# A decoder layer and a non-local block: the softmax reciprocals in one DMA, and the order of SyncE's queue

## The reference

```
def attention(q, k, v, mask):                     # 16 heads of 32 columns
    scores = einsum('bhqd,bhkd->bhqk', q, k) / sqrt(32)
    scores = scores * mask - 10000.0 * (1.0 - mask)
    return einsum('bhqk,bhkd->bhqd', softmax(scores), v)

ln  = layernorm(x, ln1_s, ln1_b)
x   = x + merge_heads(attention(split(ln @ w_qkv + b_qkv))) @ w_ao + b_ao
ln  = layernorm(x, ln2_s, ln2_b)
x   = x + merge_heads(attention(ln @ w_q, ctx @ w_kv, cross_mask)) @ w_co + b_co
x   = x + gelu(layernorm(x, ln3_s, ln3_b) @ w1 + b1) @ w2 + b2
# then a non-local block of 1x1 convolutions over x and ctx, with x added at the end
```

## Time and profile before

| what | value |
|---|---|
| median of 3 runs | 2120.47 us (2114.42 to 2125.18) |
| the profiled execution | 2126.38 us, its span 2124.4 us |
| busy PE / PEld / DVE / ACT / POOL | 95% / 75% / 69% / 55% / 26% of the span |
| mean granted TensorE clock | 0.974 |
| busy PE from 1400 us to the end of the span | 717.94 of 724 us |
| DMA packets | 670,396, of which 483,073 under 512 bytes |

### The profile page before, as it was taken

One profiled execution on the slowest core, in us unless ns is written; L12 is line 12 of the kernel. 1 busy time (PEld: TensorE's weight loads), 2 busy tenths in 40 slices (PEclk: granted clock), 3 DMA queues, 4 the chain that ended last, 5 costly groups with the idle time before them and its releaser, 6 DMA issues. The chain is left out here.

```text
span 2124.4 us, 41981 instructions
## 1 busy us (share of the span) xinstructions
PE 2010.5 (95%) x13584; PEld 1589.6 (75%) x13584; DVE 1474.8 (69%) x3874; ACT 1158.1 (55%) x3239; POOL 553.4 (26%) x562
## 2 busy tenths in 40 slices
PE   9998999999998999999999999799999999999998
PEld 8876676766766666767777767577888888888887
DVE  7798888987978877977988988566343544434333
ACT  4387777877867877877877877532111111212111
POOL 1022221221224334233333334134131303213100
PEclk9999999999999999999999999899999999999999
DMA  8445565565466665566566566552212121121201
GB/s 273 152 97 124 131 165 124 118 161 126 117 179 159 174 167 140 154 166 140 154 169 152 146 169 155 134 167 65 65 50 68 49 79 37 67 72 51 62 23 45
DMA packets 670396, 257.42 MB, mean 121 GB/s; under 512 B 483073, under 2 KB 614785, under 8 KB 670209
## 3 DMA queue, kind: packets, MB, share of 16 engines
q1 hardware_dynamic: 670208, 255.12, 46.4%
HBM read 170.56 MB, written 84.41 MB: 120 GB/s over the span
## 5 line engine op out<-in xcount | busy, mean ns | idle before, releaser
L1323 ACT ACTIVATE A_p<-A_p,A_nmax 128x256 f32<-128x256 f32 x1024 | 506.6, 500 | 1.7 <-DVE A_res L1591 1.7
L1615 DVE TENSOR_TENSOR A_p<-A_sc,A_mk 128x1024 f32<-128x1024 f32 x256 | 312.2, 1220 | 156.2 <-DMA exponentials<-A_p 80.6
L1625 DVE CUSTOM_DVE_ANT_0 A_p<-A_p,A_ma 128x256 f32<-128x256 f32 x1024 | 372.9, 418 | 4.7
L836 POOL TENSOR_TENSOR A_ct_l<-A_cx,A_ct_h 128x256 fp32r<-128x256 f32 x128 | 118.7, 927 | 725.7 <-DVE A_nmax L1625 694.6
L1330 ACT ACTIVATE A_pt<-A_tp 128x512 f32<-128x512 f32 x384 | 214.3, 589 | 124.8 <-PE A_tp L1085 124.0
L1085 PEld LDWEIGHTS A_tp<-A_ident,A_p 128*128 128x128 f32 x1536 | 185.7, 148 | 77.2 <-issue 32.3
L1085 PE MATMUL A_tp<-A_ident,A_p 128*128 128x128 f32 x1536 | 231.6, 290 | 1.1 <-DVE A_xt_l L1574 0.7
L1103 PE MATMUL A_banks<-A_pt,A_v 128*32 128x256 f32 x2048 | 151.3, 417 | 78.0 <-DMA A_pt<-exponentials 76.5
L1323 ACT ACTIVATION_READ_ACCUMULATOR A_p<-A_p,A_nmax 128x1 f32 x1024 | 196.9, 192 | 0.0
L1462 ACT ACTIVATE A_mk<-A_tp,A_cols 128x512 f32<-128x512 f32 x62 | 42.7, 689 | 269.0 <-PE A_tp L70 269.0
L1462 ACT ACTIVATE A_ma<-A_tp,A_cols 128x512 f32<-128x512 f32 x62 | 42.8, 690 | 241.4 <-PE A_tp L70 241.4
(11 more groups left out here) (247 smaller groups left out, 5074.2 us busy)
## 6 DMA issues: line engine op xcount, KB each, us to landing
exponentials<-A_p SPq DMA_DIRECT2D x512, 64.0 KB, 2.2
A_pt<-exponentials SPq DMA_DIRECT2D x128, 256.0 KB, 3.8
A_x<-x SPq DMA_DIRECT2D x96, 256.0 KB, 3.8
A_res<-x SPq DMA_DIRECT2D x64, 256.0 KB, 2.9
A_rt<-inverses SPq DMA_DIRECT2D x512, 32.0 KB, 1.9
x<-A_res SPq DMA_DIRECT2D x64, 256.0 KB, 3.4
turned<-A_x SPq DMA_DIRECT2D x240, 64.0 KB, 2.2
inverses<-A_turned_inv SPq DMA_DIRECT2D x512, 1.0 KB
```

Of the source, the lines that this page charges most:

```text
L836: pool.tensor_tensor(ct_l[:, f, part], cx[:, :], f32(ct_h[:, f, part]), ALU.subtract).then_inc(c_lo, 1)
L1323: act.activation(p[:, g % 2, j, t, :], p[:, g % 2, j, t, :], ACT.Exp, scale=-1.0, bias=nmax[:, g % 2, j, t:t + 1], accum_out=rsum[:, g % 2 ...
L1615: dve.tensor_tensor(p[:, g % 2, heads, :, :].rearrange("p j t s -> p j (t s)"), sc[:, heads, :], m, ALU.mult)\
L1625: dve.tensor_tensor_reduce(out=a_, in0=a_, in1=ma[:, b, t, :], scale=-1.0, scalar=BIG, op0=ALU.add, op1=ALU.min, accum_out=nmax[:, g % 2, ...
```

## The change

The reciprocals of a group leave `turned_inv` in one DMA over all 128 partitions, the unused columns included, and the scratch tensor in DRAM grows from 2x8x128 to 2x128x32. For this the sums are kept with the head ahead of the query tile, `rt` is filled in runs of 32 queries, with the two query tiles of a run behind each other, and `scaled` reads it in that order. In SyncE's queue, the writes of row tiles 0 and 1 (`store`) go from slot 5 to slot 6, the block writes of row tile 3 (`store_tile`) come right behind tile 2's in slot 5, and the loads of residual tiles 2 and 3 (`load_res`) go from the middle of slot 6 to its end, behind the writes.

```diff
-        rsum = room.sb("rsum", [P, 2, TPB, HPG])
+        rsum = room.sb("rsum", [P, 2, HPG, TPB])
...
                 wait_apart(sp, inv_t, grp + 1, ld_i, (grp - 1) * HPG * DMA)
-                for n in range(P // 32):
-                    sp.dma_start(inv_dram[g % 2][:, n * 32:(n + 1) * 32], turned_inv[n * 32:n * 32 + TPB * HPG, g % 2, :])\
-                        .then_inc(st_i, DMA)
+                sp.dma_start(inv_dram[g % 2], turned_inv[:, g % 2, :]).then_inc(st_i, DMA)
...
-                wait_apart(sp, st_i, (grp + 1) * (P // 32) * DMA, cx_ok, grp)
+                wait_apart(sp, st_i, (grp + 1) * DMA, cx_ok, grp)
+                blocks = inv_dram[g % 2].rearrange("(n c) s -> n (c s)", c=32).rearrange("(a n) s -> a n s", a=1)
                 for j in range(HPG):
                     rr = slice(j * HD, (j + 1) * HD)
-                    own = inv_dram[g % 2].rearrange("(t j) s -> j t s", j=HPG)[j:j + 1]
-                    sp.dma_start(rt[rr, :].rearrange("p (t s) -> p t s", t=TPB), own.broadcast_to([HD, TPB, P]))\
-                        .then_inc(ld_i, DMA)
+                    own = blocks[:, :, j * TPB * 32:(j + 1) * TPB * 32]
+                    sp.dma_start(rt[rr, :].rearrange("p (n s) -> p n s", n=P // 32),
+                                 own.broadcast_to([HD, P // 32, TPB * 32])).then_inc(ld_i, DMA)
...
                     store_inverses(r, h)
-                    if h == 6 and 0 < k < NU:
-                        for t in range(2):
-                            load_res(k - 1, r - 1, t + 2)
...
-                if by_blocks(k) and h == 4:
-                    store_tile(k, r, 0)
-                    store_tile(k, r, 1)
-                if by_blocks(k) and h == 5:
-                    store_tile(k, r, 2)
...
-                if h == (5 if k < NU else 3) and k:
+                if h == (6 if k < NU else 3) and k:
                     for t in range(2):
                         store(k - 1, r - 1, t)
-                if by_blocks(k) and h == 5:
-                    store_tile(k, r, 3)
+                if by_blocks(k) and h in (4, 5):
+                    store_tile(k, r, 2 * h - 8)
+                    store_tile(k, r, 2 * h - 7)
+                if h == 6 and 0 < k < NU:
+                    for t in range(2):
+                        load_res(k - 1, r - 1, t + 2)
...
-                dve.tensor_tensor(cx[:, :], banks[:, pv[0], 0:S], rt[:, :], ALU.mult).then_inc(cx_ok, 1)
+                in_order = lambda ap: ap.rearrange("p (t n s) -> p t n s", t=TPB, n=P // 32)
+                dve.tensor_tensor(in_order(cx[:, :]), in_order(banks[:, pv[0], 0:S]),
+                                  rt[:, :].rearrange("p (n t s) -> p t n s", t=TPB, n=P // 32), ALU.mult).then_inc(cx_ok, 1)
```

More of the change, by code:

```diff
@@ L1323, in exponential @@
                 act.activation(p[:, g % 2, j, t, :], p[:, g % 2, j, t, :], ACT.Exp, scale=-1.0,
-                               bias=nmax[:, g % 2, j, t:t + 1], accum_out=rsum[:, g % 2, t, j:j + 1]).then_inc(exped, 1)
+                               bias=nmax[:, g % 2, j, t:t + 1], accum_out=rsum[:, g % 2, j, t:t + 1]).then_inc(exped, 1)
             def turned_out(r, h, i):
@@ L1631, in inverses @@
                 dve.wait_ge(exped, (grp + 1) * HPG * TPB)
-                dve.reciprocal(rinv[:, g % 2, 0:TPB * HPG], rsum[:, g % 2, :, :].rearrange("p t j -> p (t j)"))\
+                dve.reciprocal(rinv[:, g % 2, 0:TPB * HPG], rsum[:, g % 2, :, :].rearrange("p j t -> p (j t)"))\
                     .then_inc(inv_ok, 1)
-                wait_apart(dve, inv_ok, grp + 1, st_i, (grp - 1) * (P // 32) * DMA)
+                wait_apart(dve, inv_ok, grp + 1, st_i, (grp - 1) * DMA)
                 dve.transpose(turned_inv[:, g % 2, :], rinv[:, g % 2, :]).then_inc(inv_t, 1)
@@ L1901, in decoder_layer_and_nonlocal @@
     m1t = nc.dram_tensor("m1t", [B, P, S], F32, kind="Internal").ap()
-    inverses = nc.dram_tensor("inverses", [2, TPB * HPG, P], F32, kind="Internal").ap()
+    inverses = nc.dram_tensor("inverses", [2, P, 32], F32, kind="Internal").ap()
     exponentials = nc.dram_tensor("exponentials", [2, MOVED, TPB, S, P], F32, kind="Internal").ap()
```

## The result

| | time, us | ratio to before |
|---|---|---|
| before, 12 runs beside it | 2120.83 (2114.42 to 2132.19) | |
| changed kernel, 12 runs | 2138.03 (2131.18 to 2143.32) | 1.0076, 95% interval 1.0058 to 1.0094 |

The change makes the kernel **0.76% slower**, 17 us. 2100 with 2064 to 2132 was forecast: the direction was wrong and the time lies outside the range. The profiled execution took 2137.21 us, its span 2135.3 us, at a mean granted clock of 0.973 against 0.974.

The account below looks back on a forecast made before the run. PE, 95% busy, was bounded by late A_pt loads in SyncE's queue, 6.85 us a round; 5.5 after: 19 us over 14 rounds, plus 4 elsewhere, less 3 for the clock, gives -20 us: 2100, range 2064 to 2132.

Parts of the forecast that it names:

- slot 6: Slot 6's load of A_pt goes 2.2 us earlier, at 436.2, leaving a stall of 2.3 us of 4.47.
- 0.4 + 0.9: SyncE time freed by the single reciprocal DMA ahead of slot 6's load: 0.4 us in slot 4, 0.9 in slot 5.
- the excess of 2.0 us: Slot 5's two writes took 2.91 us to issue, usually 0.83; the excess was assumed to stay, only 0.9 counted.
- The rival with 2068: Slot 5's long issue disappears too, so slot 6 hardly stalls: 3.4 us a round, about 2068; chance 0.20.
- only these two issues are that long in this slot: Argument for the rival that slot 5's excess goes too: only the two residual writes issue that long there.
- the loads of rt in smaller pieces: Four loads in pieces of 256 bytes instead of 512: at most 0.3 us later landing, on VectorE's scaling; taken as 0.
- The write lands 3.4 us after its issue.: End of slot 6: the first residual load waits for this landing and goes at 445.5, slot 7's A_pt load at 446.5.
- fourth rival: Slower: slot 6's write lands late behind the 512 KB load and PE's clock falls; about 2146, chance 0.22.
- the third term: Clock: a slow stretch in slot 7 mostly runs into the wait; charged 0.2 us a round, 3 us.
- the second term: After slot 7's weighing: 0.6 us of PE idle for the next block, 0.4 us for VectorE's lateness in slots 0 and 1.

Follow-up runs that it names:

- `swap_only`: `one_dma` with the four block writes of row tile 3 ahead of the two residual writes in slot 5, slot 6 as before; 2095.99 us, ratio 0.9883.
- `one_dma`: The kernel before with only the reciprocals changed to one DMA, SyncE's queue in the order of before; 2095.21 us, ratio 0.9883.
- `pair_behind`: The changed kernel with slot 6's 512 KB load moved from ahead of the two writes to between them and the residual loads; 2104.23 us, ratio 0.9924.
- `gap_behind`: `pair_behind` with row tile 0's four block writes right behind slot 4's load of A_pt, in SyncE's idle time; 2081.59 us, ratio 0.9827.
- `write_early`: The changed kernel with slot 6's writes right behind the reciprocals and the residual loads behind the loads of rt; 2109.48 us, ratio 0.9947.
- `tile_in_gap`: `one_dma` with row tile 0's four block writes right behind slot 4's load of A_pt, in SyncE's idle time; 2077.36 us, ratio 0.9801.

## Why the prediction was wrong

**Right: slot 6.** From the end of slot 5 (429.12 after, 428.13 in rows 2) the load of A_pt goes at +7.83 us, forecast +8.07 (436.2), before +10.30. The stall is 2.10 us, forecast 2.3. Over 14 rounds the single DMA alone takes 20.3 us off slot 6 (61.3 to 41.0), 1.45 us a round, forecast 0.4 + 0.9.

**Right: the excess of 2.0 us stays**, on the eight writes L733 (6.12 us, where the same eight take 4.2 in slot 4 of the kernel before). The rival with 2068 is out, by `swap_only` also as an explanation. The prediction's "only these two issues are that long in this slot" holds for round 4 and five others, not for the other eight. The excess is still in slot 5 although three DMAs a slot are gone, and the page has the same 94 transfers and 1.54 MB on the instruction queue as the earlier trace rows. The Trainium skill, "Runtime: NRT & Kernel Launch", section Instruction fetch mechanics, has the crossing of a fetched block mostly hidden; whether this excess is one that isn't hidden, no run here shows.

**Right: the loads of rt in smaller pieces** cost next to nothing. Their median landing is 2.1 us (1.9 in rows 6), inside the 0.3 that was given, and `one_dma` has them and gains 27 us. The 512 bytes of the Trainium skill ("DMA: Bandwidth & Descriptors", section Specifications) decide nothing here: landing rises by 0.2 us where pieces are halved to 256 bytes.

**Wrong, the step that failed: "The write lands 3.4 us after its issue."** It landed 5.3 us after it, and slot 7's load of A_pt went at +20.18 from the end of slot 5, forecast +18.4, so PE weighed at +23.95, forecast +22.3. The 3.4 is a median over 64 writes at different places: those of slot 5 land after 3.1 us in the median, those of slot 7 after 3.9. The trace of before had a place with the neighbours of the new one: in slot 7 the writes stand directly behind two loads of 256 KB. SyncE's timeline in round 5 and the view of the two writes:

```profile
532.60 0.91 SPq L483 DMA_DIRECT2D A_x<-x  x2
533.55 0.91 SPq L501 DMA_DIRECT2D x<-A_res  x2
...
DMA to landing us min/median/max: 5.3/5.4/5.5
```

That is what the two writes of the changed kernel then took. Not every round has it so long: that place has 3.3 to 5.5 us before, and the new one 4.0 to 6.0 with a median of 4.9, and 3.4 is at the low end of the one and below the other. The 4.7 us of the first write in slot 5 of round 4, behind a 512 KB load and four small writes, is of another kind: 2.44 of them are its own long issue (2.91 for the two in the earlier trace rows).

The prediction's fourth rival said it in words ("Writes are the transfers that land latest after a 512 KB load, which stands right in front of them in slot 6") and gave it 0.22, while the forecast's sum used the median. `pair_behind` shows that this term is the loss: with the load gone from in front of the writes, slots 6 and 7 together take 21.75 us a round from the end of slot 5 ((29.5 + 25.8) / 14 + 17.8), forecast 22.3. In the changed kernel they take 23.6. These 1.3 us in 14 rounds are 18 us. That `pair_behind` comes to 2104 us, near the forecast's 2100, is in part luck: its slot 0 costs 20 us more than the forecast has, and slots 6, 7 and 1 to 5 less.

**Wrong, the second term: slot 0, "0.6 us of idle" and 0.4.** It takes 2.15 us a round above the undisturbed slot (30.1 / 14), forecast 1.0: 16 us. Of the 2.15, 0.58 had been there before (8.1 / 14), which the sum didn't look at. The step counted VectorE up to the lower half of the next block and stopped there. Its queue has one more piece that PE waits for, the drain of the second product of slot 7. It stood in the trace of before, right behind the lower half of the earlier trace rows:

```profile
453.67 0.68 DVE L1591 TENSOR_TENSOR A_res<-A_banks,A_res 128x512 f32<-128x512 f32 x1
```

GpSimd's and VectorE's timelines of the changed kernel in round 4:

```profile
450.65 2.49 POOL L790 TENSOR_TENSOR A_res<-A_res,A_o_bias 128x512 f32<-128x512 f32 x2 [11.31 <-DMA A_res<-x]
...
452.01 0.69 DVE L1586 TENSOR_TENSOR A_res<-A_banks,A_res 128x512 f32<-128x512 f32 x1 [4.03 <-POOL A_res L790]
...
454.38 1.22 DVE L1575 TENSOR_TENSOR A_xt_l<-A_e,A_xt_h 128x1024 fp32r<-128x1024 f32 x1
455.52 0.68 DVE L1586 TENSOR_TENSOR A_res<-A_banks,A_res 128x512 f32<-128x512 f32 x1
```

The second drain ends at 456.20 and PE's product begins at 456.25, with the 1.09 us of idle named after it. That is 0.6 us behind the lower half. But over the 14 rounds PE's idle time in slot 0 is only 5.5 us; most of the 30.1 us is time at the lower clock, the third term. `pair_behind` (33.8) and `gap_behind` (29.4) show that slot 0's cost doesn't come from the late write alone: it goes with the loads at the end of slot 6, since the kernels with the loads at the old place have 8.0 to 14.9, and `write_early`, with them in the middle of the slot, 17.1.

**Wrong, the third term: the clock, "0.2 us a round".** The sum took the slow stretch of slot 7 (2.38 us in rows 2) out of the round and charged 0.2 us for a new one. The stretch did not go, it moved. Slots 7 and 0 at the turn from round 3 to 4, before, then in the changed kernel, and there also at the turn from 4 to 5; the third number from the end is the granted clock:

```profile
363.35:374.48 11.13, 11.13 (x77) 8.35 (x77) 6.98 (x24) 6.21 (x17) 2.57 (x2) 0.78 0.71 177
374.48:383.38 8.90, 8.90 (x81) 6.84 (x77) 8.76 (x26) 7.42 (x25) 1.59 (x1) 1.00 0.74 192
```

```profile
359.63:371.77 12.14, 8.97 (x76) 6.92 (x77) 6.17 (x16) 8.22 (x26) 2.45 (x2) 1.00 0.73 188
371.77:384.36 12.59, 12.03 (x77) 9.09 (x77) 10.93 (x35) 6.76 (x19) 2.19 (x3) 0.73 0.60 155
...
453.07:463.32 10.25, 9.16 (x77) 6.92 (x77) 10.12 (x34) 6.14 (x19) 1.37 (x2) 1.00 0.70 178
```

From the granted clock of every slot of rounds 1 to 14 I work out, as an estimate, how long it stood at the lower level: before 18 us in slot 6, 67 in slot 7 and none in slot 0, together 85; in the changed kernel 7, 20 and 47, together 74. Slot 0 has it in 11 of the 14 rounds. PE's work takes about twice its time there (1.93 us for 1.07), so 47 us are up to 24 us lost. The three slots 0 without it, of rounds 1, 5 and 9, take 10.53, 10.25 and 11.02 us, the 11 with it 11.17 in the mean.

How the clock and the drain share the 16 us isn't shown, since each hides the other: a slow PE comes later to the product and waits less for it. `gap_behind` has only 14 us at the lower level in slot 0, but 19.4 us of idle, and its slot 0 is as long.

The rival's mechanism was right (write and load took 1.7 us more: 5.3 to landing and 2.7 from L497 at 447.95 to GpSimd's start at 450.65, for 3.4 + 2.9), and so was its fall of the clock, which comes in the slot behind the stall. Its price of 2146, 8 us above the median, charged 2.4 us a round for it; the slots 0 above, only three of them at the full clock, put it at some 0.6 us a round beside the wait that it hides.

**Together:** the forecast for the profiled execution was 2106, it took 2137, 31 us more. 18 us in slots 6 and 7 and 16 in slot 0 are 34, less the 3 that had been charged for the clock. Two smaller misses cancel: slots 6, 7 and 0 of the kernel before hold 100.6 us in these rounds and not 6.85 x 14 = 96, and 4 us arose outside them.

## What to carry to other kernels

A landing time belongs to a place in the queue, not to a kind of transfer: before a DMA is put in front of something that waits for it, look what stands ahead of it there and take the landing from a place with the same neighbours, or from the longest of the rows (2.0 to 5.5 us over the 64 writes before, median 3.4). See too that the time counts from the start of the issue, and take a long issue off. Where a write and the load into its room must follow each other, leave other issues between them and nothing large ahead. And where a queue is the bound in one slot, look first for its idle time in the slots before: moving four DMAs 7 us earlier into a gap of 2 us brought 18 to 21 us. The slow stretch of the clock behind a stall wants the same care as a wait: work out where it comes to lie after the change before taking it out of the sum.

## What was not expected of the hardware

Landings of 256 KB transfers from one queue, each by what was issued ahead of it: 2.6 us for the writes of `pair_behind`, with the small loads of rt ahead; 5.3 us for the same writes directly behind a load of 512 KB, and 5.4 before behind two of 256 KB; 6.7 us for a load behind 1 MB of loads (two of 256 KB, one of 512 KB). The transfer times of part 6 are medians that hide this.

Idle time alone doesn't tell whether and when TensorE's clock falls. In slot 7 of the changed kernel the weighing ran at the lower level (1.93 or 1.94 us) behind all idle times of 3.77 us and more and at the upper one behind those of 2.30 us and less; between them it did both: rounds 2, 3 and 6 had 1.07 us behind 3.25, 3.17 and 3.25 us, rounds 10, 11 and 5 the lower level behind 3.10, 3.38 and 3.47. For rounds 2, 3 and 6 the fall only came later: the slot 0 behind them has a granted clock of 0.84, 0.73 and 0.84. In `tile_in_gap` one wait of 2.14 us was enough, and in round 8 of `pair_behind` one of 3.52 us in slot 6 was not: that slot and the one behind it stand at 1.00.
